# Stacked q and k with zero rows up to 128, and the heads' tile over the last quarter of W1

## The reference, cut to what matters

```python
qkv = jnp.einsum('bnc,ec->bne', x, w_qkv)
qkv = qkv.reshape(B, N, 3, H, D).transpose(2, 0, 3, 1, 4)
q, k, v = (qkv[0], qkv[1], qkv[2])
attn = jnp.einsum('bhid,bhjd->bhij', q, k) * SCALE
attn = jax.nn.softmax(attn, axis=-1)
out = jnp.einsum('bhij,bhjd->bhid', attn, v)
```

## Time and profile before

| | us |
| --- | --- |
| median of 3 runs | 4402.16 |
| lowest and highest | 4379.66, 4405.91 |
| profiled execution | 4418.51 |
| its span, first to last instruction | 4416.7 |
| PE busy (share of the span) | 3398.2 (77%) |
| PEld busy | 3035.2 (69%) |
| DVE busy | 2136.5 (48%) |
| ACT busy | 1404.5 (32%) |
| POOL busy | 361.6 (8%) |
| mean granted clock of TensorE, share of 2.4 GHz | 0.805 |

### The profile page before, as it was taken

How to read it: one execution, slowest core, us unless ns; L and a number is a source line. 1 busy time by engine, 2 the same in 40 slices (tenths; PEclk the granted TensorE clock), 3 DMA queues, 4 the chain that set the end, 5 groups by cost and what they waited for, 6 DMA issues and landing times.

```text
span 4416.7 us, 63033 instructions
## 1 busy us (share of the span) xinstructions
PE 3398.2 (77%) x23190; PEld 3035.2 (69%) x23190; DVE 2136.5 (48%) x5286; ACT 1404.5 (32%) x2904; POOL 361.6 (8%) x746
## 2 busy tenths in 40 slices
PE   5778777777787777887777877777778777787767
PEld 4767776677776676776666777667677666677655
DVE  4454454545454445455444445444545545544433
ACT  2333333233333333333233333323333323233321
POOL 1010000000010001000001000000000000100000
PEclk8778888778887788787777787877888878778778
DMA  4332322233222233222233232223322223322222
GB/s 116 74 75 64 75 64 52 47 74 71 68 65 55 44 75 74 64 70 50 47 72 74 64 75 64 50 50 74 74 66 68 52 44 75 74 64 65 54 40 54
DMA packets 101366, 284.55 MB, mean 64 GB/s; under 512 B 24183, under 2 KB 65416, under 8 KB 90317
## 3 DMA queue, kind: packets, MB, share of 16 engines
q1 hardware_dynamic: 101324, 283.99, 28.3%
HBM read 189.87 MB, written 15.00 MB: 46 GB/s over the span
## 4 chain that ended last, share of the span: by engine, by line
PE 54%; DVE 22%; DMA 8%; issue 8%; ACT 3%; POOL 2%; SPq 1%; DVEq 0%; POOLq 0%; ACTq 0%
PE banks L634 24%; PE banks L678 10%; PE banks L777 6%; DMA stack<-low 6%; PE banks L810 4%; PE banks L796 4%; DVE inv L1052 4%; DVE hx L946 4%; PE banks L658 2%; DVE nmax L1041 2%; DVE stats L934 2%; DVE xnT L972 2%; POOL rstd L580 2%; DMA stack<-nmaxT 2%; ACT xnT L1182 1%
## 5 line engine op out<-in xcount | busy, mean ns | idle before, releaser
L777 PE MATMUL banks<-stack 64*99 64x198 f32 x1536 | 326.2, 383 | 325.9 <-issue 187.7
L777 PEld LDWEIGHTS banks<-stack 64*99 64x99 f32 x1536 | 270.6, 273 | 378.6 <-issue 208.3
L1041 DVE TENSOR_REDUCE nmax<-banks 99x4 f32<-99x788 f32 x384 | 358.1, 975 | 289.4 <-PE banks L777 289.4
L634 PE MATMUL banks<-xnT,fc_wT 128*128 128x198 f32 x1920 | 442.3, 419 | 42.1 <-DVE xnT L972 42.1
L634 PEld LDWEIGHTS banks<-xnT,fc_wT 128*128 128x128 f32 x1920 | 415.8, 328 | 60.9 <-DVE xnT L972 51.3
L1182 ACT ACTIVATE xnT<-banks 128x396 fp32r<-128x396 f32 x192 | 96.2, 501 | 946.9 <-PE banks L658 946.9
L796 PE MATMUL banks<-stack 65*99 65x198 f32 x1536 | 284.5, 316 | 120.0 <-DMA stack<-nmaxT 98.2
L578 POOL TENSOR_TENSOR var_eps<-moments,eps 99x2 f32<-99x2 f32 x256 | 51.6, 201 | 3890.3 <-DVE moments L939 3890.3
L678 PE MATMUL banks<-w_sb,hidT 128*99 128x192 f32 x1536 | 351.1, 394 | 0.0
L796 PEld LDWEIGHTS banks<-stack 65*99 65x99 f32 x1536 | 223.6, 212 | 178.1 <-issue 127.0
L946 DVE TENSOR_SCALAR hx<-hx,moments,rstd 99x192 f32<-99x192 f32 (+1 forms) x768 | 247.3, 384 | 161.4 <-POOL rstd L580 157.7
(11 more groups left out here) (188 smaller groups left out, 5453.9 us busy)
## 6 DMA issues: line engine op xcount, KB each, us to landing
w_sb<-w_split SPq DMA_DIRECT2D x64, 1536.0 KB
xin<-in_x_dram SPq DMA_DIRECT2D x32, 1176.0 KB
w_sb<-in_L_ffn_W_dram SPq DMA_DIRECT2D x64, 576.0 KB, 6.7
stack<-hi SPq DMA_DIRECT2D x64, 297.0 KB, 4.9
stack<-hi SPq DMA_DIRECT2D x128, 148.5 KB, 6.0
stack<-low SPq DMA_DIRECT2D x128, 148.5 KB, 7.0
stack<-low SPq DMA_DIRECT2D x64, 297.0 KB, 8.8
out_dram<-y SPq DMA_DIRECT2D x64, 73.5 KB
```

The source lines that it names most:

```text
L634: last = t_.matmul(dst, a, b, start=(j == 0), stop=(j == len(pairs) - 1))
L777: last = t_.matmul(b[n % 4][0:R, t * SP_:(t + 1) * SP_], stack[p][0:SLOT, block_of(n, 0), t * R:(t + 1) * R], stack[p][0:SLOT, block_of(n, ...
L1041: v.tensor_reduce(nmax1[p][:, :, 4 * j:4 * j + 2].rearrange("p t h -> p h t"), src, AX, ALU.max, negate=True).then_inc(nmax1_ready[p], 1)
```

## The change

- q gets tiles of its own, `q_stack`, 128 rows by 12 heads by 198 columns. Its rows from 64 on are set to zero once (DVE). k's tile, `k_stack`, has 128 rows too and is the first part of a tile `shared`, in which W1's first three quarters lie; k's rows from 65 on hold what W1 left there, and meet q's zeros. The maximum and the score pass take all 128 rows.
- Row 64 of `q_stack` holds the negative maxima during the score pass, so for each image a small transfer sets it to zero again (from 12 zero rows), and the maxima and the ones go out as two transfers.
- SP sends q's part at `qk1_0` (two high, the zero row, two low transfers) and k's at `qk1_1` (two high, two low). All are of 148.5 KB but the zero row.
- W1's last quarter is a tile `w1_last`, loaded by a transfer of its own, and `headT` lies over it.
- The order of the maxima in `nmax1` is changed to q's 12 and then 12 ones.
- `STAGED` is 2.

```diff
-STAGED = 3
+STAGED = 2
...
+        q_stack = [sb(f"q_stack{p}", [128, HEADS, SP_], F32R) for p in range(2)]
...
+            shared = two("shared", [128, HEADS * SP_], F32R)
             for p in range(2):
-                with ExitStack() as weights:
-                    w1_sb.append(sb(f"w1_sb{p}", [128, 2, 2, F], F32R, weights))
-                stack.append(sb(f"stack{p}", [SLOT + 1, 2 * HEADS, SP_], F32R, loop))
+                w1_sb.append(shared[p][:, 0:3 * F].rearrange("p (a f) -> p a f", a=3))
+                k_stack.append(shared[p][:].rearrange("p (h s) -> p h s", h=HEADS))
+                with ExitStack() as heads:
+                    headT.append(sb(f"headT{p}", [128, GROUPS, SP_], stack=heads))
+                w1_last.append(sb(f"w1_last{p}", [128, F], F32R, loop))
...
-                if name == "qk1_1":
-                    sp.wait_ge(hi_ready[p], 2 * it + 2)
...
+                if name in ("qk1_0", "qk1_1"):
+                    j = int(name[4])
...
+                    sp.wait_ge(hi_ready[p], 2 * it + 1 + j)
+                    sp.dma_start(dst[0:HD], high).then_inc(stacked[p], 16)
+                    sp.dma_start(dst[(2 - j) * HD:(3 - j) * HD], high).then_inc(stacked[p], 16)
+                    if j == 0:
+                        sp.dma_start(q_stack[p][SLOT:SLOT + 1].bitcast(F32), q_stack[p][128 - HEADS:, 0, :].bitcast(F32)).then_inc(stacked[p], 16)
+                    sp.wait_ge(low_ready[p], 2 * it + 1 + j)
+                    sp.dma_start(dst[(1 + j) * HD:(2 + j) * HD], rest).then_inc(stacked[p], 16)
+                    sp.dma_start(dst[3 * HD:SLOT], rest).then_inc(stacked[p], 16)
                 if name == "maxT":
                     sp.wait_ge(nmaxT_ready[p], it + 1)
-                    sp.dma_start(stack[p][SLOT:SLOT + 1].bitcast(F32), nmaxT[p][:].bitcast(F32)).then_inc(nmax_placed[p], 16)
+                    sp.dma_start(q_stack[p][SLOT:SLOT + 1].bitcast(F32), nmaxT[p][0:HEADS].bitcast(F32)).then_inc(nmax_placed[p], 16)
+                    sp.dma_start(k_stack[p][SLOT:SLOT + 1].bitcast(F32), nmaxT[p][HEADS:].bitcast(F32)).then_inc(nmax_placed[p], 16)
...
-                        pe.wait_ge(stacked[p], 96 * it + 96)
+                        pe.wait_ge(stacked[p], 144 * it + 144)
...
-                                             stack[p][0:SLOT, block_of(n, 0), t * R:(t + 1) * R],
-                                             stack[p][0:SLOT, block_of(n, 1), :], start=True, stop=True)
+                                             q_stack[p][:, n, t * R:(t + 1) * R], k_stack[p][:, n, :], start=True, stop=True)
...
-                            pe.wait_ge(nmax_placed[p], 16 * it + 16)
+                            pe.wait_ge(nmax_placed[p], 32 * it + 32)
...
-                                             stack[p][:, block_of(s, 1), kt * R:(kt + 1) * R],
-                                             stack[p][:, block_of(s, 0), :], start=True, stop=True)
+                                             k_stack[p][:, s, kt * R:(kt + 1) * R], q_stack[p][:, s, :], start=True, stop=True)
...
+                v.memset(q_stack[p][SLOT:].bitcast(F32), 0.0)
```

More of the change, by code:

```diff
@@ L227, in vit_kernel @@
             turned = [probs[p][0][:, 1, :, :] for p in range(2)]
-            headT = two("headT", [128, GROUPS, SP_])
             y = two("y", [R, T, D])
@@ L821, in stages @@
                     pe.wait_ge(xnT_ready[p], norm_count(4, it))
-                    hidden(p, 1, int(name[5]), fc1_wT, lambda c: slice(c * 128, (c + 1) * 128))
+                    hidden(p, 1, int(name[5]), lambda c: columns(fc1_wT, slice(c * 128, (c + 1) * 128)))
                 elif name[:4] == "out1":
@@ L875, in _ @@
             for p in range(2):
+                v.memset(q_stack[p][SLOT:].bitcast(F32), 0.0)
+            for p in range(2):
                 v.memset(probs0[p][:, :, SEQ:SP_], 0.0)
```

42 lines of the change are left out of this document (20 added, 22 removed).

## The result

The changed kernel takes 4172.5 us (median of 4 runs, 4168.6 to 4175.7), the kernel before 4400.5 us in the same comparison: a ratio of 0.949, 95% interval 0.9457 to 0.9522, so 228 us or 5.1% less. The profiled execution took 4169.5 us.

The account below looks back on a forecast made before the run. Bound: TensorE work in program order, broken by waits for transfers that VectorE and ScalarE have just fed. 3.3 us times 32 turns, 106 us, less 5 at the start, gave 4301 us from the 4402.2 median; 8-in-10 range 4210 to 4365 us.

Parts of the forecast that it names:

- The waits: Ahead of the maximum passes: sending q's part earlier shortens image 1's wait by 2.2 us and image 0's by 0.5 us.
- rival 3: Stack transfers go by packets, not bytes, 3.4 us more for each image: slower, 4519 us; chance 0.05.
- Filled rows at one clock: Maximum and score products: 128 rows at an unchanged clock cost 0.2 us of a turn, at most 0.4.
- The start: Once, before the loop: two staging buffers instead of three cost 5 us.
- The clock in image 1's pass: Maximum pass to score pass: the clock rises 6.3 us after the start instead of 12.4, gaining 1.1 us.
- rival 1: The clock stays high through image 1's maximum pass after the shorter wait: 83 us more gained, 4218 us; chance 0.18.
- The clock elsewhere: Image 0's score pass gains 0.5 us from an earlier clock rise; the rest of the turn had no term.
- the sum: Gain of one turn: 2.2 + 1.1 + 0.5 + 0.5 - 0.8 - 0.2 = 3.3 us, times 32 turns 106 us.
- The second transfer of the maxima: Ahead of image 0's score pass: two transfers instead of one cost 0.8 us, bounds 0 and 0.84.
- The forecast's own range: From the bounds of the forecast's terms: 4255 to 4345 us.
- Rival 2: Filled rows do nothing to the clock, busy time alone decides: 54 us less 5 gained, 4353 us; chance 0.17.

Follow-up runs that it names:

- kernel of 4111 us: Changed kernel with q's zero row put back after the scores and k's row of ones sent from a constant with k's stack; 4111.1 us.
- late transfers: Changed kernel with all the stack's transfers sent at `qk1_1`, behind k's high part, as before the change; 4284.7 us with filled rows, 4492.3 us with 64 and 65.
- the unfilled early kernel: The kernel of 4111 us with 64 rows in the maximum pass and 65 in the score pass; 4279.6 us.

## Why the prediction was right in sign and wrong in size

- **The waits: right.** 2.2 and 0.5 us were forecast, 2.63 and 0.77 came. The time from the first issue to image 1's pass is 12.4 us (2026.86 to 2039.28 in the trace after), as the 12.1 us of before said; rival 3, transfers that go by packets, which put it 3.4 us later, is out.
- **Filled rows at one clock: right.** Minimum and maximum of a product are those of before within a few ns, and the first eight products at the high clock take 0.98 us with 128 rows and 0.95 us with 64.
- **The start: right as far as one trace can tell,** 4.4 us beside 5.
- **The clock in image 1's pass: the step that failed.** The prediction let the first 6.4 us run at 1.2 GHz "as now" and put the rise 6.3 us after the start. In the turn shown the rise came near where it was put, 5.9 us after the start, but that is luck: the pass began at 2.4 GHz, with 2.91 us of waiting ahead of it instead of 5.54, and the rise ended a low stretch of little over 3 us that began inside the pass. So 2.33 us were gained instead of 1.1, where rival 1 gave 3.2. More than half of what rival 1 adds here came. That rival was set aside because a wait of 4.05 us had been followed by the low clock; 2.91 and 3.24 us were not. No wait by itself decides, though. Image 0's pass waits 3.4 us in the runs with 65 and with 96 rows alike, and its first eight products take over 1.3 us, as at the low clock, in 30 of 32 turns of the first and in 2 of the second. And after 3.24 us image 0's pass of the changed kernel began at the high clock, while in the kernel of 4111 us image 1's pass began at the low one after 3.15 us, as its timeline has it:

```profile
2001.44 1.62 PE L788 MATMUL banks<-shared,q_stack 128*99 128x198 f32 x8 [3.15 <-issue]
```

- **The clock elsewhere: missing from the sum.** Image 0's score pass gained 1.14 instead of 0.5 us, and the rest of the turn, put at nothing, 1.08 us. That rest begins with image 1's score pass, whose products have 128 rows now, and it was put at nothing without a reason; in the traces it has 13.5 us per turn at the low clock instead of 14.8. The table's gains come to 7.9 us of a turn, 4.6 more than the sum's 3.3. The three clock terms are 2.95 of these 4.6 us (1.23 in image 1's pass, 0.64 in image 0's score pass, 1.08 in the rest), the waits 0.7, the second transfer 0.8, and 0.2 is the price of the rows, which has no line of its own in the table.
- **The second transfer of the maxima: a wrong size, and a wrong kind of price.** Its wait was put at 3.9 us and is 3.38; 0.31 us more than before, not 0.8. The issue is no quicker (0.80 us), but a transfer of half the size lands sooner: alone, in the kernel of 4111 us, it takes 2.21 us from its issue to the score pass (1979.47 to 1981.68), where the whole one took 2.65. But its price is not the wait alone: with late transfers and without the fill it cost 85 us, mostly with the clock, and together with the zero row it still costs 61 us in the changed kernel.
- **By parts:** the prediction gave the earlier transfers 2.7 us of a turn, 86 us, and the runs 122. It gave the rows 1.6 us, 51 us, and the runs 138, with up to 31 more from both together. The rows' share was the one that was mis-sized most.
- **The forecast's own range: a slip.** The bounds that it names lie 0.5, 0.8 and 1.1 us above its terms, 2.4 us of a turn together, so its lower end is 4224 us and not 4255. The measured time is below that too, since the rest of the turn and the longer gain of the waits stood in no bound.
- **Rival 2, the fill does nothing to the clock: out.** With the same count and columns of products and the same transfers, 169 us are gained where the number of rows is the only edit (4280 to 4111). The Trainium skill, "TensorE: Matmul & The Clock Gate", "Part 1: The HAM clock gate", ties the clock to how busy the array is and names no rows. The trace of the unfilled early kernel disagrees, with busy time as the profile counts it, as the one of before did: busy 9.80 of 9.80 us at 0.50. (In the 12.00 us at 0.50 that the prediction reads, 24 of 59 products have 64 rows, not quite half.)

What stays open: why one small pause moves the clock by so much and not always the same way. With 128 rows the two small transfers on the path cost 61 us; with 64 and 65 rows and early transfers the kernel that has them is the faster one (4247 beside 4280 us). The three waits of a turn are 9.3 us together in the first and 9.1 in the second, and what differs is how long the clock is low, 39.3 and 43.9 us of a turn. By the Trainium skill, the same page and section, the chip's look at the array's activity runs freely and does not start anew with a kernel, so that the same pause could fall differently from case to case; no run here tests it. The five turn lengths are open as well, and with them how much of each difference belongs to an edit and how much to the step that it fell on.

## What to carry to other kernels

Where a profile shows TensorE busy all the time at 1.2 GHz and the instructions there use half of the rows, count the low stretch as a cost of the thin operands, and try filling the rest with zeros. Here a product cost at most some 4 ns more for it (0.98 instead of 0.95 us for eight). Cost an edit near such a stretch by the whole stretch, not by its own tenths: a second small transfer that made a wait 0.77 us longer took 85 us. Before you size an edit by the difference of two runs, look at the length of a turn in both: kernels with different edits had the same turn here. And put a small transfer at the end of its group or behind the consumer; at the head of the queue it delayed all the others (56 us).

## What the hardware showed that was not expected

- A granted clock of 0.50 with TensorE busy 9.80 of 9.80 us on 64-row products among 128-row ones. The kernel's time by the number of rows alone: 4280 with 64 and 65, 4274 with 65, 4168 with 96, 4111 with 128; the same 4168 came with 128 rows in the maximum pass alone.
- Turns of quite different kernels keep to five lengths from 119.5 to 133.1 us (414 of 459 turns within 0.4 us).
- Filled rows in a pass that shortens nothing alone (the score pass, 0 to 3 us) are worth 58 to 97 us once the other pass is filled.
- Extra products, most of them in idle time, went with more low clock elsewhere: 18.9 instead of 9.9 us per turn in the last part of a turn, and 177 us more in all.
